# Output projection of an RWKV block as products of high and low parts, in a two-stage kernel with a mixture of experts

## What is computed

```python
x = x + attn(_layernorm(x))
x = x + moe(_layernorm(x))
...
r, k, v = (xr @ Wr.T), (xk @ Wk.T), (xv @ Wv.T)   # by head: 16 heads of 16 channels
g = jax.nn.gelu(xg @ Wg.T, approximate=False)
att = rc @ kc
yc = att * Wmat @ vc + rc @ state * wb
new_state = ws * state + kc * wk @ vc
...
yn = (y - mean) / jnp.sqrt(var + EPS)             # mean and variance of each head
yn = yn * ln_w + ln_b
out = yn * g @ Wo.T                               # the output projection
```

## Time and profile before

| what | value |
|---|---|
| median of 3 runs | 849.97 us (848.99 to 852.12) |
| profiled execution | 843.76 us |
| its span, first to last instruction | 841.8 us |
| mean granted TensorE clock | 0.992 of full speed |
| TensorE busy | 813.4 us (97%), 6343 products |
| VectorE busy | 498.2 us (59%) |
| ScalarE busy | 490.0 us (58%) |
| POOL busy | 460.8 us (55%) |

### The profile page before, as it was taken

How to read it: one execution, slowest core, us unless ns; L and a number is a source line. 1 busy time by engine, 2 the same in 40 slices (tenths; PEclk the granted TensorE clock), 3 DMA queues, 4 the chain that set the end, 5 groups by cost and what they waited for, 6 DMA issues and landing times. The chain is left out here.

```text
span 841.8 us, 17487 instructions
## 1 busy us (share of the span) xinstructions
PE 813.4 (97%) x6343; PEld 679.4 (81%) x6343; DVE 498.2 (59%) x1237; ACT 490.0 (58%) x876; POOL 460.8 (55%) x497
## 2 busy tenths in 40 slices
PE   4899999999999999899999999999999999999997
PEld 3678888788788777778998788899788899788886
DVE  6888889899897776343543543544443545353441
ACT  4578888888888788264543543644552544453331
POOL 5454476778777766475444356453446452535215
PEclk9999999999999999899999999999999999999999
DMA  4852032113111121556333334342415442413114
GB/s 151 331 214 70 28 108 85 60 52 97 40 46 47 66 92 65 173 156 136 101 70 40 111 96 69 96 113 27 124 65 74 121 107 27 99 33 43 22 13 51
DMA packets 50475, 74.05 MB, mean 88 GB/s; under 512 B 5057, under 2 KB 42177, under 8 KB 50369
## 3 DMA queue, kind: packets, MB, share of 16 engines
q1 hardware_dynamic: 35488, 53.46, 19.4%
q0 software_dynamic: 14592, 19.18, 13.7%
q10 hardware_dynamic: 288, 0.01, 0.0%
HBM read 38.41 MB, written 34.22 MB: 86 GB/s over the span
## 5 line engine op out<-in xcount | busy, mean ns | idle before, releaser
L1593 POOL DMA_INDIRECT out<-ysb,index x80 | 124.6, 1558 | 145.9 <-DVE ysb L1832 112.1
L1946 PE MATMUL p<-xh,whi 128*128 128x512 f32 (+2 forms) x504 | 185.5, 368 | 0.5 <-PEq L1494 0.4
L1948 PE MATMUL p<-xh,wlo 128*128 128x512 f32 (+2 forms) x504 | 185.2, 368 | 0.0
L1808 DVE TENSOR_TENSOR hid<-gated,p 128x512 f32<-128x512 f32 (+1 forms) x126 | 81.1, 643 | 175.0 <-ACT gated L1655 175.0
L1947 PE MATMUL p<-xl,whi 128*128 128x512 f32 (+2 forms) x504 | 184.6, 366 | 0.0
L1972 PE MATMUL py<-w,hh 128*128 128x512 f32 x448 | 163.3, 404 | 3.9 <-DVE hl L1089 3.3
L1655 ACT ACTIVATE gated<-p 128x512 f32<-128x512 f32 (+1 forms) x126 | 70.9, 563 | 156.1 <-PE p L1948 156.1
L1582 POOL TENSOR_TENSOR wlo<-wraw,whi 128x448 fp32r<-128x448 f32 x56 | 70.8, 1267 | 88.7 <-ACT whi L1641 81.6
L1946 PEld LDWEIGHTS p<-xh,whi 128*128 128x128 f32 x504 | 94.7, 188 | 18.0 <-issue 2.5
L1971 PE MATMUL py<-w,hl 128*128 128x256 f32 x384 | 108.9, 284 | 0.0
L1947 PEld LDWEIGHTS p<-xl,whi 128*128 128x128 f32 x504 | 94.8, 188 | 15.1
(11 more groups left out here) (204 smaller groups left out, 1444.1 us busy)
## 6 DMA issues: line engine op xcount, KB each, us to landing
wraw<-in_w SPq DMA_DIRECT2D x24, 896.0 KB, 5.0
disp<-wraw SPq DMA_DIRECT2D x16, 662.5 KB, 8.9
xtok<-disp SPq DMA_DIRECT2D x16, 530.0 KB, 4.8
x_ring<-in_x SPq DMA_DIRECT2D x16, 256.0 KB, 3.8
out<-x SPq DMA_DIRECT2D x16, 256.0 KB, 2.2
xtok<-disp SPq DMA_DIRECT2D x8, 265.0 KB, 4.1
out<-ysb,index POOLq DMA_INDIRECT x80, 3.8
disp<-row,slot_i POOLq DMA_INDIRECT x64
```

Of the source, the lines that this page charges most:

```text
L1593: nc.gpsimd.indirect_dma_start(out, bass.IndirectOffsetOnAxis(ap=index[e.const % 2][:, t:t + 1], axis=0), ysb[j % NY][:], None, compute_op ...
L1808: nc.vector.tensor_tensor(hid[k][:, 0:w], gated[k][:, 0:w], p3[k][:, 0:w], ALU.mult).then_inc(hid_ready, 1)
L1946: nc.tensor.matmul(dst[:, 0:w], hi[m][:, wcut], xh[xcut], start=(kt == 0), stop=False)
L1948: ins = nc.tensor.matmul(dst[:, 0:w], lo[m][:, wcut], xh[xcut], start=False, stop=(kt == KT - 1))
```

## The change

The output projection becomes three fp32r products of high and low parts, as in the second stage. Wo is loaded into the tile z and split once, by ScalarE (`out_high`) and POOL (`out_low`). For each block, POOL multiplies by the gate in place (z), ScalarE rounds the result to fp32r (`gated_high`, `zg_hi`), and POOL subtracts (`gated_low`, `zg_lo`). The normed heads are written over grstd, and the tile yn goes. The ring of x has six buffers. On TensorE, `project_o` moves behind `logits`, and `group_sums` behind `project_v`; on ScalarE, `value` moves ahead of `group_log`.

```diff
-RING = 7
+RING = 6
...
-    w_in_sb = [t[:] for t in kept.w_in_sb] + [sb("w_in_sb4", [P, KT, C])[:]]
-    WV, WO = w_in_sb[2], w_in_sb[4]
+    w_in_sb = [t[:] for t in kept.w_in_sb]
+    WV = w_in_sb[2]
+    wo_hi, wo_lo = [sb(f"wo_{n}", [P, KT, C], F32R) for n in ("hi", "lo")]
...
-    yn = sb("yn", [P, KT, W])
     z = sb("z", [P, KT, W])
-    zg = sb("zg", [P, KT, W])
+    zg_hi, zg_lo = [sb(f"zg_{n}", [P, KT, W], F32R) for n in ("hi", "lo")]
...
-        sp.dma_start(WO, weights[4].rearrange("(k p) c -> p k c", p=P)).then_inc(late_in, 16)
+        sp.dma_start(z[:], weights[4].rearrange("(k p) c -> p k c", p=P)).then_inc(late_in, 16)
...
         def gated(b):
             if 0 <= b < STEPS:
                 pool.wait_ge(z_ready, b + 1)
                 pool.wait_ge(gT_ready, b + 1)
-                wait(pool, wo_done, b)
-                nc.gpsimd.tensor_tensor(zg[:], z[:], gT[b % 2][:], ALU.mult).then_inc(zg_ready, 1)
+                nc.gpsimd.tensor_tensor(z[:], z[:], gT[b % 2][:], ALU.mult).then_inc(zg_ready, 1)
+
+        def gated_low(b):
+            if 0 <= b < STEPS:
+                pool.wait_ge(zhi_ready, b + 1)
+                wait(pool, wo_done, b)
+                nc.gpsimd.tensor_tensor(zg_lo[:], z[:], zg_hi[:].bitcast(F32), ALU.subtract).then_inc(zlo_ready, 1)
+
+        def out_low():
+            pool.wait_ge(whi_o_ready, 1)
+            nc.gpsimd.tensor_tensor(wo_lo[:], z[:], wo_hi[:].bitcast(F32), ALU.subtract).then_inc(wlo_o_ready, 1)
...
             gated(c - 1)
+            gated_low(c - 1)
...
                 empty_rows()
+                out_low()
...
         gated(14)
+        gated_low(14)
...
         gated(15)
+        gated_low(15)
...
-                wait(act, yn_ready, b)
+                wait(act, z_ready, b)
                 nc.scalar.activation(grstd[:], pX[:], ACT.Ln, scale=1.0 / N, bias=gn_eps[:, 0:1]).then_inc(grlog_ready, 1)
...
+        def gated_high(b):
+            if 0 <= b < STEPS:
+                act.wait_ge(zg_ready, b + 1)
+                wait(act, wo_done, b)
+                nc.scalar.copy(zg_hi[:], z[:]).then_inc(zhi_ready, 1)
+
+        def out_high():
+            act.wait_ge(late_in, 16 * NLATE)
+            nc.scalar.copy(wo_hi[:], z[:]).then_inc(whi_o_ready, 1)
...
-            group_log(c - 1)
             value(c)
+            group_log(c - 1)
+            if c == 0:
+                out_high()
...
             receptance(c + 1)
+            gated_high(c - 1)
             pairs(c + 1)
...
         scaled(14)
+        gated_high(14)
...
         scaled(15)
+        gated_high(15)
...
-                wait(dve, z_ready, b)
-                nc.vector.tensor_tensor(yn[:], y[:], grstd[:], ALU.mult).then_inc(yn_ready, 1)
+                nc.vector.tensor_tensor(grstd[:], y[:], grstd[:], ALU.mult).then_inc(yn_ready, 1)
...
         def project_o(b):
             if 0 <= b < STEPS:
-                pe.wait_ge(zg_ready, b + 1)
+                pe.wait_ge(zlo_ready, b + 1)
                 pe.wait_ge(xT_ready, min(b + 3, STEPS))
...
-                        ins = nc.tensor.matmul(pX_tok[:, t, :], zg[:, c, t * Q:(t + 1) * Q], WO[:, c, :],
-                                               start=(c == 0), stop=(c == KT - 1))
+                        hi, lo = [part[:, c, t * Q:(t + 1) * Q] for part in (zg_hi, zg_lo)]
+                        nc.tensor.matmul(pX_tok[:, t, :], hi, wo_hi[:, c, :], start=(c == 0), stop=False)
+                        nc.tensor.matmul(pX_tok[:, t, :], hi, wo_lo[:, c, :], start=False, stop=False)
+                        ins = nc.tensor.matmul(pX_tok[:, t, :], lo, wo_hi[:, c, :], start=False, stop=(c == KT - 1))
...
             turn2(c - 2)
-            project_o(c - 1)
             logits(c - 2)
             if c == -1:
                 project_v(0)
                 turn_k(0)
             else:
+                project_o(c - 1)
                 turn_k(c + 1)
+                project_v(c + 1)
                 group_sums(c)
-                project_v(c + 1)
```

More of the change, by code:

```diff
@@ L414, in phase_a @@
     z_ready, zg_ready, wo_done = sem("z_ready"), sem("zg_ready"), sem("wo_done")
+    zhi_ready, zlo_ready, whi_o_ready, wlo_o_ready = sem("zhi_ready"), sem("zlo_ready"), sem("whi_o_ready"), sem("wlo_o_ready")
     x1_ready, stat2_ready, rstd2_ready = sem("x1_ready"), sem("stat2_ready"), sem("rstd2_ready")
@@ L788, in scaled @@
                     act.wait_ge(late_in, 16 * NLATE)
-                wait(act, zg_ready, b)
+                if b == 0:
+                    act.wait_ge(wlo_o_ready, 1)
+                wait(act, zlo_ready, b)
                 for k in range(KT):
-                    ins = nc.scalar.activation(z[:, k, :], yn[:, k, :], ACT.Identity,
+                    ins = nc.scalar.activation(z[:, k, :], grstd[:, k, :], ACT.Identity,
                                                scale=lnw_sb[:, k:k + 1], bias=lnb_sb[:, k:k + 1])
@@ L809, in on_scalar @@
             logit_exp(c - 3)
+            value(c)
             group_log(c - 1)
-            value(c)
+            if c == 0:
+                out_high()
             turned1(c + 1)
@@ L1306, in project_o @@
             if 0 <= b < STEPS:
-                pe.wait_ge(zg_ready, b + 1)
+                pe.wait_ge(zlo_ready, b + 1)
                 pe.wait_ge(xT_ready, min(b + 3, STEPS))
                 if b == 0:
-                    pe.wait_ge(late_in, 16 * NLATE)
+                    pe.wait_ge(wlo_o_ready, 1)
                 for t in range(TPS):
                     for c in range(KT):
-                        ins = nc.tensor.matmul(pX_tok[:, t, :], zg[:, c, t * Q:(t + 1) * Q], WO[:, c, :],
-                                               start=(c == 0), stop=(c == KT - 1))
+                        hi, lo = [part[:, c, t * Q:(t + 1) * Q] for part in (zg_hi, zg_lo)]
+                        nc.tensor.matmul(pX_tok[:, t, :], hi, wo_hi[:, c, :], start=(c == 0), stop=False)
+                        nc.tensor.matmul(pX_tok[:, t, :], hi, wo_lo[:, c, :], start=False, stop=False)
+                        ins = nc.tensor.matmul(pX_tok[:, t, :], lo, wo_hi[:, c, :], start=False, stop=(c == KT - 1))
                 ins.then_inc(wo_done, 1)
```

## The result

The changed kernel takes **882.98 us** (median; 881.95 to 887.1), the kernel before, beside it, 850.3 (848.99 to 852.12): a ratio of 1.0394 (95%: 1.037 to 1.0418), 32.7 us slower. The forecast was 871.8, 21.8 slower. The profiled execution after takes 883.75 us (span 882.0, mean granted clock 0.982 against 0.992), that of before 843.76, 6.5 under its median; so the two traces lie 40.0 us apart, 7 us more than the medians.

What follows compares the result with a forecast made beforehand. TensorE was taken to bound a first-stage step, VectorE next. 14.8 (order) + 4 (step 14) + 3 (end) = 21.8 us on the median 849.97 gave 871.8 us; own range 864 to 878, held 857 to 885.

Steps and rivals of the forecast that it cites:

- the step of 19.2 to 19.6: Sign of being right: first-stage steps take 19.2 to 19.6 us from turn2 to turn2.
- the idle time in front of the residual: Sign of being right: VectorE idles longer in front of the residual, by 1.2 us or so.
- One sign of being wrong: Listed as showing the forecast wrong: the granted clock falls in the middle of the stage.
- Order, 12 x 1.23 = 14.8: Logits ahead of project_o uncovers the x2T copy, delaying the residual: 1.23 us in each of twelve loop steps, 14.8 us.
- the longer of the two loops: VectorE's loop from residual to masks, 19.44 us a step, taken over TensorE's alone, 18.77 us.
- Hidden in c = 1 to 12: POOL's extra subtraction and wait, 1.97 us a step, fit its 3.9 us of idle time and cost nothing.
- rival 2: POOL's moved work holds VectorE up, 0.8 us in eight steps: 6.2 us more, 878 us; chance 0.12.
- rival 3: TensorE's clock falls at the gap before logits, 1.7 us a fall: 894 us every step, 879 every third; chance 0.10.
- Step 14, 4: POOL's product comes late at step 14, delaying cast and x2T to 5.7 us: 4 us (0.6 to 4.7).
- the end, 3: At the stage's end the last two project_o wait on product, cast and subtraction: 3 us (0 to 4).
- Start-up "free": Splitting Wo once, while ScalarE and POOL are idle in the start-up, was put at no cost.
- Products, 0.29 less a step: On TensorE, project_o's twelve fp32r products take 1.44 us instead of 1.73 for eight fp32 passes: 0.29 us less.

Runs made afterwards that it cites:

- run 2: Kernel before with only the order changed, logits ahead of project_o on TensorE: 903.12 us, ratio 1.061.
- run 3: Changed kernel without POOL's subtraction for zg_lo, the third product taking the high part again: 910.5 us, ratio 1.0712.
- run 9: Kernel before with logits ahead of project_o, and POOL's decay of the receptance ahead of its first scatter: 880.93 us, ratio 1.0354.
- run 12: Kernel before with logits ahead of project_o, and POOL's first scatter waiting for TensorE's counts ahead of turn2: 876.11 us, ratio 1.0311.
- run 4: Changed kernel with eight more products of 256 columns a step filling the gap between turn2 and logits: 880.36 us, ratio 1.0352.
- run 1: Changed kernel with the order undone, project_o ahead of logits again on TensorE, all else kept: 869.89 us, ratio 1.0229.
- run 11: Changed kernel, order undone, zg_lo subtraction moved to VectorE behind state_b, POOL's first scatter waiting for TensorE's counts: 872.27 us, ratio 1.0243.
- run 5: Changed kernel with the order undone and without POOL's subtraction for zg_lo: 860.44 us, ratio 1.0118.
- run 7: Changed kernel without POOL's subtraction for zg_lo, with eight products a step filling the gap between turn2 and logits: 891.38 us, ratio 1.0485.
- run 8: Kernel before with logits ahead of project_o, and four fp32 products a step filling the gap between turn2 and logits: 889.77 us, ratio 1.046.

## Why the prediction was right, and where its sizes failed

The sign, the range (857 to 885) and the main mechanism held. The forecast's own range (864 to 878) did not: the size was 11 us short by the medians, 18 by the traces from which its terms come (40.0 against 21.8). Of the signs that it named, the gap in front of logits, project_o at 1.5 us and the wait of 2.28 us for the last zg_lo came; the step of 19.2 to 19.6 came in c = 3 to 5 alone, and the idle time in front of the residual grew by 0.64 us at c = 8, not by 1.2. One sign of being wrong came too: the granted clock fell in the middle of the stage, in c = 6 and 12. In the two traces, from the turn2 of c = 2 to that of c = 14, the change costs 249.95 - 219.98 = 29.97 us; forecast were 14.8 and step 14 on top.

- **Order, 12 x 1.23 = 14.8.** Right. c = 3 to 5 show 19.46 against 19.44, that is 1.25 each, 15.0 in twelve. Logits at 1.36, residual at 3.97, the longer of the two loops taken; its three parts are 3.98, 14.61 and 0.88 at c = 3, put at 3.77, 14.87 and 0.8. That the order cost no more is luck: the sum knew of no late signals. Runs 2 and 3, with the same order and POOL's scatter ahead of turn2, have them; here the subtraction on POOL moves the scatter behind turn2. The order alone gives 19.86 to 20.03 (runs 9 and 12, c = 2 to 4), 1.7 more than 18.2, with the longer fp32 products.
- **"Hidden in c = 1 to 12", POOL.** This step failed. POOL's work was set against POOL's idle time, 3.9 us a stretch, and not against the VectorE instructions that it holds up. It is rival 2's mechanism, priced at 0.8 in eight steps, 6.2. Measured over 19.46: 0.67, 0.62, 1.07, 1.03 and 0.64 in c = 7 to 11, and by run 4, at the full clock, 0.82 and 0.65 in c = 6 and 12: 5.5 (at c = 8 the row product's 0.80 instead of 0.18 is the whole 0.62), of which c = 6 and 10 had 1.4 before the change, so that the change brought 4.1. The rival's mechanism was right and its size near, its chance of 0.12 too low; the row of 0.57 instead of 0.18 had shown it. What the prediction held against it, that a VectorE instruction that comes first goes ahead, is not what run 1 shows. Another 0.7 lies in c = 2 (20.14 in run 4): there z, POOL's product, the cast and x2T all come 0.9 us later against turn2 than at c = 3, and logits start at 2.25; why they do stays open.
- **The clock, rival 3.** It was given every step or every third at 1.7 us a fall. It fell in three of twelve: 3.2 + 2.1 + 2.1 = 7.3, by comparison with run 4.
- **Step 13**, 22.38 against 18.20: not in the forecast, 2.9 over 19.46. In it POOL runs the scatters of two blocks, and beside the second the signals of the outer and head products come 2.3 to 3.5 us behind their start, so that VectorE stands 2.20 us in front of kvm; the steps of runs 1, 4 and 11 are as long (22.3 to 22.5), with the same signals late. VectorE's row:

```profile
312.68 0.29 DVE L1001 TENSOR_TENSOR kvm<-pA,parity 128x128 f32<-128x128 f32 x1 [2.20 <-remote]
```

- These make 15.0 + 5.5 + 0.7 + 7.3 + 2.9 = 31.4, less 1.4 for the two longer steps of before: 30.0.
- **Step 14, 4, and the end, 3.** Step 14 grew by 2.06 (17.99 against 15.93); signals are late in it too, by 1.1 to 2.9 us, beside the next block's scatters. The path that was priced there, product, cast, x2T, is not what cost it: POOL's product starts 2.7 us ahead of turn2 instead of 0.7 behind it, step 13 being longer, and x2T is copied from 1.23 on, not done at 5.7. Behind it the stage loses 4.9 to the last turn2, 29.31 us against 24.42 from turn2(13) on; 2.5 of these are a fall of the clock (14.36 us against 11.89 in run 4). 2.06 + 2.4 is inside the bounds, for the step by luck; the sum was 7. With the 30.0 above and the 2.0 of the start-up, the 2.06 and 4.9 make 38.9 of the 40.2 us by which the spans differ.
- **Start-up "free".** turn2 of c = 2 starts 2.0 us later. It was set at nothing; run 1, which has the same start-up, is 1.9 late there.
- **Products, 0.29 less a step.** Right as busy time: with the order undone, TensorE is busy 17.93 at c = 3 instead of 18.21. The step stays at 18.19, so that none of it was gained.

What the sum could not show is that the terms don't add. The order alone costs 52 us and the rest of the change alone 19; both together 33. Each moves the other's collision away: with the new order VectorE's slots come 1.9 us later against turn2 and miss POOL's decay (0.18 us at 199.15 in the changed kernel against 1.66 in run 1), and with zg_lo on POOL the scatter starts behind turn2 instead of ahead of it.

## What to carry to other kernels

Of work put on an engine with idle time, ask which instructions behind it move, and what they will then stand beside: here, in run 1, 2 us more on POOL cost VectorE 2.3 us a step through operations that the change did not touch. A kernel that is written out by hand holds by its alignment, so undo the parts of a change one at a time and in pairs before adding their prices. Read a long step beside its neighbours (with and without scatter, with and without weight splitting) before you read a mean.

## What the runs showed of the hardware

TensorE's signals can come late while it works on. In run 5 at 163 us those of the last head products and turn2 came 1.6 to 2.5 us behind their products, and that of project_o, behind them on the same engine, at the usual 0.33. The held signals leave in order: in run 2 at c = 6 those of products begun at 152.22, 152.78 and 153.25 come at 154.82, 154.88 and 154.94. Only TensorE's were late: in c = 4 to 13 of runs 2, 3, 5, 7 and 8, ScalarE's for kT and VectorE's for the mixing, in the same microseconds, come 0.01 us behind their ends. In the loop of all these runs this came only beside POOL's scatters (c = 2 and 3, which have none, have no late signal in any run), and moving the scatter moved or removed it; but the kernel before has the same overlap (-0.97 us) and no late signal. What else it takes stays open; the profile shows no difference in the microsecond ahead of it.

The same gap of 0.72 us in front of logits was followed by a fall of the granted clock in some steps and not in others: c = 3 to 5 of the changed kernel kept 1.00, c = 6 and 12 did not. At c = 2, behind a gap of 1.59 us, it fell, and with gaps of 1.3 to 2.6 us (runs 2 and 3, c = 4 to 13) in 19 of 20 steps.
